# Two-layer gated block on one core: set-ups moved into neighbouring stages, layer 0's score banks packed

## The reference

```python
x = x + tanh(g_xattn[0]) * L0_xattn(layernorm(x), ctx, ctx, mask0, ...)   # 16 heads of 16, causal
x = x + tanh(g_ffn[0])   * L0_ffn(layernorm(x), ...)                      # 32 experts, top 8, capacity 256
x = x + tanh(g_xattn[1]) * L1_xattn(layernorm(x), ctx, ctx, mask1, ...)   # 16 heads, not causal
x = x + tanh(g_ffn[1])   * L1_ffn(layernorm(x), ...)                      # 8 experts, top 2, capacity 2048
```

## Time and profile before

| | us |
|---|---|
| median of 3 runs (2112.62 to 2115.19) | 2114.45 |
| the profiled execution: its own time | 2112.23 |
| its span in the trace | 2110.4 |
| `constants` and layer 0's set-up, to the last instruction of the latter | 0 to 27.4 |
| attention 0: up to its first exp | 27.4 to 121.1 |
| attention 0: from the first exp to the last | 121.1 to 612 |
| attention 0: tail | 612 to 660 |
| experts0 | 660 to 894 |
| layer 1's set-up and what lies around it | 894 to 923.3 |
| attention 1 | 923.3 to 1597 |
| experts1 | 1597 to 2110 |

### The profile page before, as it was taken

One profiled execution on the slowest core, in us unless ns is written; L12 is line 12 of the kernel. 1 busy time (PEld: TensorE's weight loads), 2 busy tenths in 40 slices (PEclk: granted clock), 3 DMA queues, 4 the chain that ended last, 5 costly groups with the idle time before them and its releaser, 6 DMA issues. The chain is left out here.

```text
span 2110.4 us, 30079 instructions
## 1 busy us (share of the span) xinstructions
PE 1790.4 (85%) x10491; PEld 1054.6 (50%) x10491; DVE 1063.8 (50%) x2743; ACT 908.0 (43%) x1876; POOL 598.3 (28%) x577
## 2 busy tenths in 40 slices
PE   2789999999865999537899999999954999999995
PEld 1445555555534877413344444443331666666664
DVE  3446777887745444244867777778420211212121
ACT  1356766666541222113577777776730111111110
POOL 1312111210002778503211332221122233333322
PEclk9999999999986999858999999999976999999998
DMA  3444554434123788525323433331014133333314
GB/s 96 152 120 150 150 176 134 132 129 141 65 83 99 175 173 173 91 66 159 108 72 116 136 97 95 120 117 62 32 47 136 31 81 81 78 78 75 80 20 100
DMA packets 204245, 222.86 MB, mean 106 GB/s; under 512 B 33438, under 2 KB 195231, under 8 KB 203431
## 3 DMA queue, kind: packets, MB, share of 16 engines
q1 hardware_dynamic: 176458, 177.48, 27.4%
q0 software_dynamic: 27648, 43.60, 10.9%
HBM read 155.06 MB, written 86.93 MB: 115 GB/s over the span
## 5 line engine op out<-in xcount | busy, mean ns | idle before, releaser
L873 DVE TENSOR_REDUCE nmx<-mxb 128x1 f32<-128x512 f32 (+1 forms) x896 | 522.7, 609 | 282.5 <-PE mxb L686 146.6
L741 ACT ACTIVATE pt<-stb 128x512 f32<-128x512 f32 (+3 forms) x1024 | 501.0, 519 | 266.3 <-PE stb L702 140.8
L686 PE MATMUL mxb<-kst,qst 96*128 96x512 bf16 (+4 forms) x1024 | 332.3, 346 | 30.2 <-DVE nmx L873 21.3
L699 PE MATMUL stb<-qst,kst 99*128 99x512 bf16 (+4 forms) x1024 | 342.4, 345 | 14.8 <-DMA qst<-m3T 8.4
L713 PE MATMUL ob<-pt,va 128*32 128x512 f32 (+3 forms) x2048 | 233.7, 528 | 3.8 <-ACT oT L746 2.8
L1428 PE MATMUL e_h_bank<-e_xT,e_w 128*128 128x512 f32 x512 | 226.0, 600 | 6.1 <-ACT e_xT L1468 5.4
L699 PEld LDWEIGHTS stb<-qst,kst 102*128 102x128 bf16 (+1 forms) x1024 | 100.1, 99 | 258.1 <-ACT pt L741 167.3
L1442 PE MATMUL e_y_bank<-e_w,e_h 128*128 128x256 f32 x1024 | 226.9, 379 | 0.0
L1442 PEld LDWEIGHTS e_y_bank<-e_w,e_h 128*128 128x128 f32 x1024 | 192.9, 190 | 31.8 <-issue 7.2
L1123 POOL TENSOR_TENSOR qk<-qk,parts 128x512 f32<-128x512 f32 x64 | 72.8, 1160 | 432.8 <-ACT qk L774 225.7
L1582 POOL DMA_INDIRECT x_after_l<-e_y,e_token x64 | 99.6, 1556 | 281.7 <-DVE e_y L1547 267.0
(11 more groups left out here) (231 smaller groups left out, 2493.1 us busy)
## 6 DMA issues: line engine op xcount, KB each, us to landing
qk_parts<-parts SPq DMA_DIRECT2D x16, 1536.0 KB, 6.2
qst<-qk_parts SPq DMA_DIRECT2D x384, 64.0 KB, 2.3
kst<-qk_parts SPq DMA_DIRECT2D x384, 64.0 KB, 2.3
e_w<-in_L_ffn_w SPq DMA_DIRECT2D x16, 1024.0 KB, 7.4
rows<-rows SPq DMA_DIRECT2D x15, 1060.0 KB, 8.6
crow<-in_ctx SPq DMA_DIRECT2D x16, 512.0 KB, 3.9
x_after_l<-xres SPq DMA_DIRECT2D x16, 512.0 KB, 3.2
e_gu_nat<-in_L_ffn_gate_up_proj SPq DMA_DIRECT2D x64, 128.0 KB
```

What stands on the lines that cost most here:

```text
L686: last = pe.matmul(out, qst[par][0:rows_used, h, qt * P:(qt + 1) * P], kst[par][0:rows_used, h, 0:nk], start=True, stop=not causal)
L699: last = pe.matmul(out[:, q0:S], kst[par][0:ROWS, h, kt * P:(kt + 1) * P], qst[par][0:ROWS, h, q0:S], start=True, stop=not causal)
L741: act.activation(pt[:, u % 8, q_from(kt):S], stb[(STEPS * b + u) % N_ST][:, q_from(kt):S], ACT.Exp, scale=SCALE).then_inc(s["st_free"], 1)
L873: last = dve.tensor_reduce(nmx[:, qt, h:h + 1], got[:, at:at + k_to(qt)], AX.X, ALU.max, negate=True)
```

## The change

Four things, in the order of the program.

1. `constants` and layer 0's set-up have no blocks of their own. Their instructions stand in attention 0's block. SP first issues the loads of item 0 (x and ctx), then weights, biases, gates and the rest. DVE does the casts ahead of its loop and the set-up's chain at iteration -2. PE does the set-up's products at iteration -2. The three `va` memsets go from DVE to POOL, at iteration -2.
2. Layer 1's weights and tiles belong to a new class `Layer`, made before `experts0`, and its set-up is spread over the experts: SP's loads at experts 1 and 2, PE's products at experts 4 to 9, DVE's pieces at experts 0 to 26, each after that expert's `result` of the one before. Attention 1's block begins with its first load.
3. In layer 0 the transposed scores are packed: ten banks of 512 full columns per group of four heads (40 per item) instead of sixteen of differing width (64). kt 0 has a bank per head, kt 3 and kt 1 share one (128 and 384 columns), and kt 2 of two heads share one. The mask products stay 64 per item.
4. `values` is called twice per group (at u = 10 for kt 0, at u = 18 for kt 1, 3 and 2) and not four times; `pt` has ten slots and not eight; `stb` keeps three banks.

Three of a group's four value calls now stand in one row, behind the exps of the whole group. The diff, cut to its core:

```diff
-        @block.sync
-        def _(sp):
-            sp.dma_start(c.gates[:, 0:2], g_xattn.partition_broadcast(P)).then_inc(gate_in, 16)
-            sp.dma_start(c.gates[:, 2:4], g_ffn.partition_broadcast(P)).then_inc(gate_in, 16)
-            sp.wait_ge(empty_set, 2)
-            sp.dma_start(rows1[0:SPARE, :].rearrange("(t p) w -> p t w", p=P), empty[:, :, :]).then_inc(empty_out, 16)
-            sp.wait_ge(empty_out, 16)
...
+def constants_vector(c, dve, ii, empty):
+    dve.memset(empty, 0.0).then_inc(c.made, 1)
...
+    dve.wait_ge(c.iota_s, 1)
+    dve.wait_ge(c.made, 2)
+    dve.tensor_copy(empty[:, :, D:D + 1], ii[:, 200:200 + SPARE // P].unsqueeze(2)).then_inc(c.empty_set, 1)
+    dve.wait_ge(c.iota_s, 2)
...
+    dve.tensor_copy(c.slot_at[:, :, :], ii[:, 128:128 + n].rearrange("p (e s) -> p e s", e=E1)).then_inc(c.made, 1)
+    dve.wait_ge(c.made, 3)
+    dve.wait_ge(c.tables, 2)
...
+def score_banks(packed):
+    banks = {}
+    for g in range(GROUPS):
+        if not packed:
+            banks.update({16 * g + u: ((4 * g + u % 4, u // 4, 0),) for u in range(16)})
+            continue
+        for j, u in enumerate((0, 2, 3, 5)):
+            banks[16 * g + u] = ((4 * g + j, 0, 0),)
+        for j, u in enumerate((7, 8, 10, 11)):
+            banks[16 * g + u] = ((4 * g + j, 3, 0), (4 * g + j, 1, P))
+        for j, u in enumerate((13, 15)):
+            banks[16 * g + u] = ((4 * g + 2 * j, 2, 0), (4 * g + 2 * j + 1, 2, 2 * P))
+    return banks
...
+    PACKED = causal
...
+    VALUE_CALLS = {10: (0,), 18: (1, 3, 2)} if PACKED else {6: (0,), 10: (1,), 14: (2,), 18: (3,)}
...
+            if layer == 0:
+                for w, s_ in ((wq, wq_s), (wk, wk_s), (wv, wv_s)):
+                    sp.dma_start(s_[:, :, :], w.rearrange("(c p) n -> p c n", p=P)).then_inc(a.w_in, 16)
...
+                constants_sync(c, sp)
...
+                empty_store(c, sp, empty)
...
+            if layer == 0:
+                constants_gpsimd(c, pool, ii)
             for it in ITERATIONS:
+                if layer == 0 and it == -2:
+                    for i in range(3):
+                        last = pool.memset(va[i][:, :, :, :], 1.0)
+                    last.then_inc(a.va_ones, 1)
...
+                if e == 1:
+                    for w, s_ in zip((wq, wk, wv, wp), nat):
+                        sp.dma_start(s_[:, :, :], w.rearrange("(c p) n -> p c n", p=P)).then_inc(a.w_in, 16)
...
+            def set_up(e):
+                if e == 0:
+                    dve.memset(a.m3T[0][:, :], 1.0).then_inc(a.stack_ones, 1)
+                elif e < 4:
+                    dve.memset(a.va[e - 1][:, :, :, :], 1.0)
...
+                    if e == 2:
+                        dve.memset(a.mask3[:, :], 0.0).then_inc(a.zeroed, 1)
+                    if e == 3:
...
+                        dve.tensor_scalar(a.mask3[0:3, :], mrow_i, 0.0, None, ALU.not_equal).then_inc(a.m_t, 1)
+                elif e < 7:
+                    dve.wait_ge(a.w_t, e - 3)
+                    dve.tensor_copy((a.wq, a.wk, a.wv)[e - 4][:, :, :], put_b[:, :].rearrange("p (c n) -> p c n", c=NC)).then_inc(a.w_put, 1)
...
                 if e > 0:
                     result(e - 1)
+                set_up(e)
```

More of the change, by code:

```diff
@@ L246, in shared_banks @@
     return banks
-def attention(c, layer, x_in, ctx_in, mask, wq, bq, wk, bk, wv, bv, wp, bp, wroute, x_out, rows,
+def score_banks(packed):
[11 more added lines that the diff above has]
+    return banks
@@ new lines, with split_bias @@
+N_SPLIT = 8
+def split_bias(c, dve, a, dst, src, h, link, before):
+    if link > 0:
+        dve.wait_ge(a.b_chain, before + link)
+    if link in (0, 2, 4):
+        last = dve.tensor_copy(h[link // 2], src)
+    elif link in (1, 3):
+        last = dve.tensor_tensor(src, src, h[link // 2], ALU.subtract)
+    elif link == 5:
+        last = dve.tensor_scalar(dst[0:3, :], h[0], c.ident[0:3, 0:1], None, ALU.mult)
+    else:
+        last = dve.scalar_tensor_tensor(out=dst[0:3, :], in0=h[link - 5], scalar=c.ident[0:3, link - 5:link - 4],
+                                        in1=dst[0:3, :], op0=ALU.mult, op1=ALU.add)
+    last.then_inc(a.b_chain, 1)
@@ L250, in attention @@
+def attention(c, layer, a, x_in, ctx_in, mask, wq, bq, wk, bk, wv, bv, wp, bp, wroute, x_out, rows,
               qk_dram, mask_dram, tot0=None, token=None):
@@ L692, in scores @@
             def scores(b, u):
-                par, g, kt, j = b % 2, u // 16, u % 16 // 4, u % 4
+                par = b % 2
                 if u % 32 == 0:
                     pe.wait_ge(s[f"shift_in{u // 32}"], 48 * (b + 1))
-                wait(pe, s["st_free"], STEPS * b + u - N_ST + 1)
-                q0, h = q_from(kt), 4 * g + j
-                out = stb[(STEPS * b + u) % N_ST]
-                last = pe.matmul(out[:, q0:S], kst[par][0:ROWS, h, kt * P:(kt + 1) * P],
-                                 qst[par][0:ROWS, h, q0:S], start=True, stop=not causal)
@@ L701, in scores @@
-                if causal:
-                    last = pe.matmul(out[:, q0:q0 + P], c.identb[:, :], c.hide_st[:, :], start=False, stop=True)
+                if u not in SCORE_BANKS:
+                    return
+                no = N_SCORE * b + SCORE_NO[u]
+                wait(pe, s["st_free"], no - N_ST + 1)
+                bank = stb[no % N_ST]
+                for h, kt, at in SCORE_BANKS[u]:
+                    to = at if PACKED else q_from(kt)
+                    last = pe.matmul(bank[:, to:to + S - q_from(kt)], kst[par][0:ROWS, h, kt * P:(kt + 1) * P],
+                                     qst[par][0:ROWS, h, q_from(kt):S], start=True, stop=not causal)
+                    if causal:
+                        last = pe.matmul(bank[:, to:to + P], c.identb[:, :], c.hide_st[:, :], start=False, stop=True)
@@ new lines, in values, with set_up @@
+                last.then_inc(s["pt_free"], 1)
+            def set_up():
+                pe.wait_ge(a.l_in, 80)
+                for cc in range(NC):
+                    last = pe.transpose(stb[0][:, cc * E0:(cc + 1) * E0], route_nat[:, cc * P:(cc + 1) * P], c.ident[0:E0, 0:E0])
+                last.then_inc(a.w_t, 1)
+                pe.wait_ge(a.bv_rdy, 2)
+                for ci in range(NC):
+                    last = pe.matmul(ob[0:3, 0:D], bv3[:, ci, :], wp_s[:, ci, :], start=ci == 0, stop=ci == NC - 1)
+                last.then_inc(a.bv_out, 1)
```

528 lines of the change are left out of this document (293 added, 235 removed).

## The result

The changed kernel takes 2086.29 us (median of 4 runs, 2081.89 to 2094.81) against 2114.82 for the kernel before in the same comparison: a ratio of 0.9869, 95% interval 0.9848 to 0.9889, so 28.5 us less. The forecast was 2068, range 2054 to 2084, so the time lies 2.3 us above the range. The direction was right, the size was not: 61% of the gain came. The profiled execution took 2089.91 us with a span of 2088.2, 22.2 less than the span before.

A forecast was written before the change was run, and what follows sets the result against it. No engine bounds the whole: stages have a limit each (PE in layer 0's exp stretch, POOL in experts0). 2112.23 - 21.2 + 4.5 - 22.2 - 7 = 2066.3; the median 2.2 above gives 2068 us, range 2054 to 2084.

The forecast's parts named there:

- the packing term: Layer 0's attention: fewer value calls and lighter exps save 7 us; bounds 0, if DVE takes all back, and -15.
- Start: Program start: item 0's statistics 21.2 us earlier, POOL's memsets costing 4.5 back, so first exp 16.7 us earlier.
- the cover: Start of attention 0: PE's set-up products and DVE's 9.6 us chain hide under POOL's 4.5 us delay; otherwise DVE costs 1 to 3.
- Layer 1's set-up: Ahead of attention 1: its first load moves to where the set-up's first load stood, -22.2 us.
- Experts0: Spread set-up pieces beside POOL, which sets the pace: 0, up to +3 us if experts 2 and 3 do not catch up.
- rival 3: Experts0: POOL's indirect DMAs stand still while DVE works in SBUF, up to 19.34 us longer, 2087 us; chance 0.05.
- Both parts of my sum: Layer 0's attention: half the value calls go, 5.8 us, and PE's 4.2 us of waits for ACT's exps mostly go.
- Rival 5: Layer 0's attention: the second value call stops PE at every group's end, making the kernel slower than before; chance 0.03.
- Rival 4: Program start: the first set-up is not hidden, the start's 16.7 us are lost, 2085 us; chance 0.05.
- Rival 2: Layer 0's attention and start: packing pays nothing and POOL's memsets cost the two-operand price, 2082 us; chance 0.16.
- the four signs: Tanh after 12 us; POOL memsets above 4; experts0 adds over 6.7 apart; PE waiting for exps at every second value call.

The follow-up runs named there:

- the second: The kernel before, unchanged, traced again: 2113.59 us (one run).
- e8_all_tail: The changed kernel with layer 1's whole set-up (loads, PE's and DVE's pieces) behind the last expert instead of spread: 2087.72 us, ratio 0.9886 to the kernel before.
- e5: The changed kernel, still packed, with DVE taking layer 0's score maxima over half the columns: 2054.78 us, ratio 0.9723 to the kernel before.
- e6: The changed kernel with layer 0's scores unpacked and maxima over half the columns: 2061.39 us, ratio 0.9754 to the kernel before.
- e3: The changed kernel with the ten packed score banks of a group on other steps: 2085.57 us, ratio 0.9850 to the kernel before.
- e7_start: The changed kernel with gates' DMAs first, POOL's memsets at program start, and DVE's second chain half behind item 1's statistics: 2074.12 us.
- e9_gap: e7_start with the memsets between item 0's norm1 and rest of q, the mask's cast out of experts0 and its fill at expert 27: 2070.67 us.

## Why the prediction was wrong

The step that failed is the packing term: its 7 us did not come. The start and experts0 missed by less. In the program's order, packing last:

**Start: nearly right in size, wrong inside.** Forecast -16.7; -14.0 against the first trace, -17.7 against the second. Tanh came at 10.19 and not 9.0, so the statistics gained 20.1 of 21.2 us. A memset cost 1.76 and not the 2.24 that I took (with which my own terms add up to +4.8 and not +4.5); the Trainium skill's "GPSIMD Engine Reference", section 4.1, with its one-input rate near VectorE's, was the better price. The step that failed here is the cover: I let DVE's chain hide under POOL's delay at its old length of 9.6 us, and its second half alone took 12.6, mostly because POOL's memsets held it up. POOL waited 3.49 us for it. From the rest of q to the rest of k POOL took 15.06 us and before 8.09, so 7.0 more and not 4.5.

**Layer 1's set-up: right.** From the last add to attention 1's first load -22.05 for -22.2. The 2.5 us that the stage lost after that go with the clock: from the first load to the first exp the granted clock is 0.76 on average, over 923.3 to 1024.5 it was 0.79 before, and in the thirteen traces that stretch runs from 99.0 us at 0.81 to 105.8 at 0.75. The first maximum had kept the full gain (974.2 to 950.7, 23.5 us).

**Experts0: the range was too small.** Forecast 0 to +3, measured +5.0 and +2.8 against the two traces. The late evacuations came as said (DVE's copies of e_xT at 685.56 and 692.62 follow its set-up pieces without a gap); not in the sum was the gather that stood still under DVE's cast of the mask. That is rival 3 at one place and not along the whole stage: the adds go on at 1.63 and 1.58 us. The Trainium skill ("SBUF — State Buffer", "Who interferes with whom") names just this: a cast or tensor_scalar of VectorE in a two-port mode contends with GpSimd, and whoever issues first has the shared ports for the whole instruction while the other blocks. The trace agrees that one stands still (2.91 instead of 1.05 beside a cast of 2.28). My rival 3 told that rule in one direction only; the start paid for the other, POOL's memsets that stopped DVE (5.06 instead of 0.28).

**Packing: the step that failed.** Forecast -7 with bounds 0 and -15; in the table the way grew by 7.8 us. That is 14.8 of the 23.7 us by which the traces miss the forecast, in two parts. The larger, 8.5, is the clock, for which the sum had no term: in e8_all_tail, with the clock full up to the last exp, the same code takes 537.0. So packing itself came to about nothing: -0.7 us against the first trace of before and +1.5 against the second, which both have some half clock of their own. The other, 6.3, is that the 7 us were not there. Both parts of my sum were real: PE's work fell by 1.4 us an item (0.7 forecast) and its waits for exps by 2.5 us in all. The error was to price them on an engine with 95% of busy time over a whole item. The item has parts with different limits. In the second head group DVE set the pace before already; in the first DVE, 90% busy, was close behind a PE that hardly waited. There the work taken from PE is given back as waits for maxima and other results: a steady item takes 68.2 us and not 65.6. I had written that DVE "takes all back" as the worst end; nothing excluded more. That the gain exists behind DVE is what e5 and e6 show (1.7 us longer with whole maxima, 0.65 shorter with half). What makes DVE late in the packed order stays open: the steps explain 0.6 us (e3), operations that meet POOL's lengthen DVE's work by 1.2, and the row of three value calls was not tested by itself.

**The rivals.** Rival 5 did not come: values waited 1.0 us for exps in all. Rival 4 did not either, and rival 3 at one place only, though their times of 2085 and 2087 are nearest to the 2086.3 measured: that is luck. Rival 2's "packing pays nothing" was right in its first half, at 2082 by an addition that was wrong in its second, the memsets. None of the four signs that I named for being wrong appeared (tanh at 10.19, memsets of 1.76, adds 6.6 us apart, hardly a wait for exps): none of them looked at DVE's chain, at waits for maxima or at the clock.

## What to carry to other kernels

Cut a steady loop into its parts before pricing work taken from its busiest engine: an engine at 95% over the period can still wait for another in part of it, and work taken from it there comes back as waiting. Before moving a long operation to GpSimd, look what VectorE does at that time: the price is not only the operation's duration but also the chain of small operations that it stops. Before crediting a stage's difference to an edit, compare it with an execution that has the same code in that stage. An idle slot is only free if nobody waits for what the other engine does in it; the third place tried for the memsets was the first of that kind.

## What the hardware showed that was not expected

GpSimd and VectorE stopped each other for whole instructions, in both directions: casts of 4 to 128 columns took 3.45 to 3.60 us under what was left of three memsets of 1.76 each (e7_start), a cast of 3x256 took 5.06 instead of 0.28, a tensor_scalar 1.28 instead of 0.35, a gather on GpSimd 2.91 instead of 1.05, and adds on GpSimd 2.44 to 2.97 instead of 1.58 in six other kernels. VectorE's reductions from PSUM showed no such growth (686 ns for 512 columns before, 682 after). Two DMAs of 1 KB, issued first at 0.81 and 1.27 us, were seen by ACT only at 5.9 us when the loads of x and ctx followed at once (e7_start, e9_gap); alone they were there at 4.6.
